# Splitting the fp16 parts of the expert weights into halves in a decoder layer

## The chip, the cores and the metric

The kernel runs on one core of a Trainium2 chip. Its time is the device time of one execution in microseconds (us); a lower one is better. The core has five engines that run side by side and wait for each other through semaphores: PE (matmul), ACT (activations), DVE (vector work), POOL and SP (which issues DMAs).

## The reference

One decoder layer over 8 sequences of 512 tokens, 256 wide: windowed self-attention, cross attention over a context, and a mixture of 8 experts of which each token uses 2. The change touches the work that lies in the second of them, cut here to its core with the experts behind it:

```python
scores = jnp.einsum('bqd,bkd->bqk', query, key)
scores = scores - tri[None, :, :]
probs = jax.nn.softmax(scores / SCALE, axis=-1)
return jnp.einsum('bqk,bkd->bqd', probs, value)
...
x = _layernorm(x + _L0_xattn_ref(x, ctx_1024, ctx_1024), axis=-1)
...
for e in range(NUM_EXPERTS):
    w_e = jnp.sum(jnp.where(top_i == e, routing_w, 0.0), axis=-1)
    h = jax.nn.gelu(xf @ expert_w1[e].T, approximate=False)
    out = out + h @ expert_w2[e].T * w_e[:, None]
```

## The kernel before

**Stages.** Window attention fills the first 525 us or so. Then comes the cross attention, one sequence b = 0 to 7 after another, some 18 us each (about 527 to 671 us of the profiled span). Behind it stand the routing (to about 715 us) and the experts, whose matmuls fill the rest.

**Expert weights.** The experts multiply in fp16 with each weight split in two: a high part, which is the scaled weight rounded to fp16, and a low part, which is what the rounding lost. There are 8 experts with two matrices each (k = 0 and 1), 2048 values to a partition in each. While the cross attention runs, SP loads them, ACT makes the high parts (`high_part`, L993, its instruction L999) and DVE the low parts (`low_part`, L1515, its instruction L1518). High and low of (e, k) lie in the memory of the loaded weights: the high part of (e, k) is written over the second half of the loaded (e, k-1), or of (e-1, 1). So `high_part(e, k)` waits on `w_low_made` until the low parts of all matrices before it are done (L998), and `low_part(e, k)` waits on `w_high_made` for its own high part.

**Order in a sequence.** No scheduler sets it: each engine runs its instructions in the order in which they are written. Sequences 2 to 5 run in a loop whose addresses are worked out in registers on the engine; 0, 1, 6 and 7 are written out.

- PE (`attend`, L639): scores of the four row blocks t = 0 to 3 (L646), with the transposes of the previous sequence's result (L686) ahead of t = 3; the router's product (L695); then for each t the transposes of the probabilities (L661) and, one block behind, the product with the context (L672). The product q = 2 uses the PSUM bank of q = 0 again, so it waits until the first residual sum has read it (L668).
- ACT (`attend`, L953): the high part of (b-2, 1), two copies (L1004, L1008), the exponentials of t = 0 and 1 (L963), the high part of (b-1, 0), the copy of the transposed probabilities of t = 0 (`copy`, L975), then exp(2), copy(1), exp(3), copy(2), copy(3), and two copies for the next sequence (L951).
- DVE (`attend`, L1472): masks (L1476), row peaks (L1480) and their scaling (`scale_peaks`, L1485), with the low part of (b-2, 1) between `scale_peaks(0)` and `mask(3)`; the choice of experts for sequence b-1 (`choose`, L1530 to L1539); the low part of (b-1, 0); the four residual sums, each a reciprocal (L1507), the sum (L1508) and the statistics (L1511); then eight tiny instructions, POOL's root (L1168) and the norm (L1524).

The four residual sums close a sequence: the norm follows the fourth, and PE, ACT and DVE all need the norm's result in the next sequence.

Of the kernel before, what the change touches and what calls it, by code (L numbers as in the profile page):

```python
# [16 lines left out]
ALU = mybir.AluOpType  # L17
# [30 lines left out]
N_EXP, TOP, F = 8, 2, 1024  # L48
FB = F // P
EW = C * F  # L50
PIECES = CHUNK
PIECE = N_EXP * EW // PIECES
F32_BIAS, F32_MANT = 127, 23
# [59 lines left out]
def past(t, k):  # L113

    return not isinstance(t, int) or t >= k
# [12 lines left out]
def decoder_layer(nc, x, x_steps, ctx, ctx_t, Wq, Wkv, q_g, q_b, k_g, k_b, Wwin, bwin, Wout,  # L128
                  router_t, w1_t, w2_t, shape_consts, out):
    stack = ExitStack()  # L130
    with stack:
# [3 lines left out]
        def sem(name):  # L135
            return stack.enter_context(nc.semaphore(name))
# [24 lines left out]
        def next_low(phase, *shape):  # L161
            start = low_used.get(phase, 0)
            n = 1
            for m in shape:
                n *= m
            low_used[phase] = start + n
            assert start + n <= LOW, (phase, start + n)
            return carve(low, start, *shape)
# [29 lines left out]
        where8 = next_low("cross", 2, QT, 8)  # L198
        assert low_used["cross"] <= LOW - EW // 2

# [36 lines left out]

        w_f32 = carve(big, 0, N_EXP, 2, EW)
        arena16 = arena[:, :].bitcast(F16)
        w_low = arena16[:, 2 * LOW:2 * LOW + 4 * N_EXP * EW].rearrange("p (e k x) -> p e k x", k=2, x=2 * EW)  # L240
        w_high = arena16[:, 2 * LOW - EW:2 * LOW - EW + 4 * N_EXP * EW].rearrange("p (e k x) -> p e k x", k=2, x=2 * EW)
# [5 lines left out]
        w_scale = carve(mid, scale_at, 8)  # L247
# [53 lines left out]
        w_piece = next_low("window", 2, PIECE)  # L301
        w_squares = next_low("window", 2, PIECES)
        w_sum = next_low("window", 2)
# [124 lines left out]
        w_high_made = sem("w_high_made")  # L428
        w_low_made = sem("w_low_made")
# [153 lines left out]
        def _(pe):  # L583
# [140 lines left out]
            nc.tensor.transpose(psum[0:TOP * TILES, 3, 0:P], top_v.rearrange("p k t -> p (k t)"), ident).then_inc(gates_turned, 1)  # L724

            pe.wait_ge(routed, 1)
            pe.wait_ge(w_low_made, 2 * N_EXP)

            def block_of(w, e, k, at, n):

# [69 lines left out]
        def _(act):  # L800
# [151 lines left out]

            def attend(b, u, i, more=True):  # L953
                if past(b, 2):
                    high_part(b - 2, 1)

                def exp(t):
                    act.wait_ge(peak_ready, 2 * b + t // (QT // 2) + 1)
                    if t >= 2:
                        act.wait_ge(pt_done, QT * b + t - 1)  # L960
                    elif past(b, 1):
                        act.wait_ge(pt_done, QT * b + t - 1)
                    nc.scalar.activation(probs[:, t % 2, 0:(t + 1) * P], psum[:, t, 0:(t + 1) * P], ACT.Exp,  # L963
                                         bias=bias2[:, u, t:t + 1], scale=1.0 / E ** 0.5,
                                         accum_out=row_sum[:, u, t:t + 1]).then_inc(exp2_done, 1)

                def copy(t):
                    act.wait_ge(pt_done, QT * b + t + 1)
                    if t < 2 and past(b, 1):
                        act.wait_ge(router_done, b)  # L970
                    if t >= 2:
                        act.wait_ge(av_done, QT * b + t - 1)
                    elif past(b, 1):
                        act.wait_ge(av_done, QT * b + t - 1)
                    nc.scalar.activation(probs_t[:, t % 2, 0:t + 1, :], psum[:, 4 + t % 2, 0:(t + 1) * P].rearrange(  # L975
                        "p (k n) -> p k n", n=P), ACT.Copy).then_inc(pt_copied, 1)
                if past(b, 1):
                    keep_x2(b - 1, 1 - u)
                    x2_transposed(b - 1)
                exp(0)  # L980
                exp(1)
                if past(b, 1):
                    high_part(b - 1, 0)
                copy(0)
                exp(2)
                copy(1)
                exp(3)
                copy(2)
                copy(3)
                if more:  # L990
                    copy_x1t(b + 1)

            def high_part(e, k):  # L993

                act.wait_ge(w_scaled, 1)
                act.wait_ge(w_loaded, 32 * e + 32)
                if k or past(e, 1):
                    act.wait_ge(w_low_made, 2 * e + k)  # L998
                nc.scalar.activation(w_high[:, bass.ds(e, 1), k, 0:EW], w_f32[:, bass.ds(e, 1), k, :],  # L999
                                     ACT.Copy, scale=w_scale[:, k:k + 1]).then_inc(w_high_made, 1)  # L1000

            def keep_x2(b, u):
                act.wait_ge(normed2, QT * (b + 1))
# [7 lines left out]
            steps(act, B - 2, attend)  # L1011
            attend(B - 2, 0, B // 2 - 1)
            attend(B - 1, 1, B // 2 - 1, more=False)
            high_part(N_EXP - 2, 1)
            keep_x2(B - 1, 1)
            x2_transposed(B - 1)
            high_part(N_EXP - 1, 0)
            high_part(N_EXP - 1, 1)


            nc.scalar.activation(count_psum, consts[:, AT_COUNT:AT_COUNT + P], ACT.Copy).then_inc(count_beside, 1)
# [213 lines left out]
        def _(dve):  # L1235
# [236 lines left out]
            def attend(b, u, i, more=True):  # L1472
                def mask(t):
                    dve.wait_ge(s_done, QT * b + t + 1)
                    diag = psum[:, t, t * P:(t + 1) * P]
                    nc.vector.tensor_tensor(diag, diag, consts[:, AT_MASK:AT_MASK + P], ALU.add).then_inc(masked, 1)  # L1476

                def find_peak(t):
                    dve.wait_ge(masked, QT * b + t + 1)
                    nc.vector.tensor_reduce(top_peak[:, u, t:t + 1], psum[:, t, 0:(t + 1) * P], op=ALU.max,  # L1480
                                            axis=AX.X).then_inc(peak_found2, 1)
                def scale_peaks(half):
                    part = slice(half * QT // 2, (half + 1) * QT // 2)
                    dve.wait_ge(peak_found2, QT * b + part.stop)
                    nc.vector.tensor_scalar(bias2[:, u, part], top_peak[:, u, part], -1.0 / E ** 0.5, None,  # L1485
                                            ALU.mult).then_inc(peak_ready, 1)
                mask(0)
                mask(1)
                if past(b, 1):
                    norm2(b - 1, 1 - u)  # L1490
                find_peak(0)
                find_peak(1)
                mask(2)
                scale_peaks(0)
                if past(b, 2):
                    low_part(b - 2, 1)
                mask(3)
                find_peak(2)
                find_peak(3)
                scale_peaks(1)  # L1500
                if past(b, 1):
                    choose(b - 1, 1 - u)
                    low_part(b - 1, 0)
                for t in range(QT):

                    dve.wait_ge(av_done, QT * b + t + 1)
                    done(nc.vector.reciprocal(inv_row[:, u, t:t + 1], row_sum[:, u, t:t + 1]), inv2_made, QT * b + t + 1)  # L1507
                    nc.vector.scalar_tensor_tensor(x1_n[:, u, t, :], psum[:, 6 + t % 2, 0:E], inv_row[:, u, t:t + 1],  # L1508
                                                   x1_n[:, u, t, :], ALU.mult, ALU.add).then_inc(sum2_done, 1)
                    dve.wait_ge(sum2_done, QT * b + t + 1)  # L1510
                    nc.vector.bn_stats(stats2[:, u, t, :], x1_n[:, u, t, :]).then_inc(stats2_done, 1)  # L1511
                dve.wait_ge(stats2_done, QT * (b + 1))
                moments(stats2[:, u], mean2[:, u, :], rstd2[:, u, :], b)

            def low_part(e, k):  # L1515

                dve.wait_ge(w_high_made, 2 * e + k + 1)
                nc.vector.scalar_tensor_tensor(w_low[:, bass.ds(e, 1), k, 0:EW], w_f32[:, bass.ds(e, 1), k, :], w_scale[:, k:k + 1],  # L1518
                                               w_high[:, bass.ds(e, 1), k, 0:EW], ALU.mult, ALU.subtract).then_inc(w_low_made, 1)

            def norm2(b, u):
                dve.wait_ge(rstd_ready, b + 1)
# [19 lines left out]
            attend(B - 2, 0, B // 2 - 1)  # L1542
            attend(B - 1, 1, B // 2 - 1, more=False)
            norm2(B - 1, 1)
            low_part(N_EXP - 2, 1)
            choose(B - 1, 1)


# [5 lines left out]
                                         count[:, 0:N_EXP].unsqueeze(1).unsqueeze(1).to_broadcast([P, TOP, TILES, N_EXP]),  # L1554
                                         ALU.is_equal), spot_step, 1)
            nc.vector.tensor_tensor(picked, chosen[:, 0], chosen[:, 1], ALU.add).then_inc(picked_made, 1)
            low_part(N_EXP - 1, 0)
            dve.wait_ge(counted, 1)
            tile_count = psum[:, 1, 0:TILES * N_EXP].rearrange("p (t n) -> p t n", n=N_EXP)

# [61 lines left out]
            half = SLOTS // 2  # L1622
# [50 lines left out]
            def result_out(s, v, i):  # L1673
                dve.wait_ge(down_done, s + 1)
                if past(s, 4):
# [2 lines left out]
                dve.wait_ge(y_beside, s + 1)  # L1678
                nc.vector.scalar_tensor_tensor(y_rows[:, v, :], psum[:, 6 + v % 2, 0:E], gate_col[:, v, :], y_side[:, v % 2, :],  # L1679
                                               ALU.mult, ALU.add).then_inc(y_copied, 1)  # L1680
            low_part(N_EXP - 1, 1)
            dve.wait_ge(routed, 1)
            quads(dve, SLOTS, lot, 8)
            result_out(SLOTS - 3, 1, SLOTS // 4 - 1)
# [54 lines left out]
```

## Time and profile before

| | us |
|---|---|
| three runs | 1202.16, 1204.65, 1205.75 |
| median | 1204.65 |
| the profiled execution | 1203.33 |
| its span | 1201.5 |
| PE / DVE / ACT / POOL busy in the span | 942.3 / 827.6 / 460.0 / 736.1 |
| 16 instructions of `high_part` | 2.00 each |
| 16 instructions of `low_part` | 2.35 each |

Times of rows are counted from the start of the span. The profiled execution took 1.8 us more than its span. The mean granted clock of TensorE over it was 0.92; two levels occur, 1.0 (2.4 GHz) and 0.5 (1.2 GHz).

How to read it: the busy times say little here, because no engine is busy throughout. What counts in each sequence is the chain of waits through PE, ACT and DVE.

### The profile page before, as it was taken

The page shows a single profiled execution, that of the slowest core. Times are in us where ns is not written, and L with a number is a line of the kernel's source. Part 1 is how long each engine was busy: PE and PEld are TensorE (multiplying, and loading weights), DVE is VectorE, ACT ScalarE, POOL GpSimd, SP SyncE. Part 2 cuts the span into 40 slices and gives each one's busy share as a digit, 9 for nine tenths or more (in the row PEclk, how much of TensorE's full clock was granted, in tenths as well). Part 3 has the DMA queues.
Part 4 walks back from the last instruction along what each step waited for, and adds up shares of the span by engine and source line. Part 5 has one row for each costly group of instructions (what it writes and reads, how often), then busy time and mean ns, then how long its engine had stood idle before and what let it go on. Part 6 is the DMA issues. An engine that isn't in the chain of part 4 may idle for free.

```text
span 1201.5 us, 24876 instructions
## 1 busy us (share of the span) xinstructions
PE 942.3 (78%) x8007; PEld 756.7 (63%) x8008; DVE 827.6 (69%) x1264; ACT 460.0 (38%) x1055; POOL 736.1 (61%) x496
## 2 busy tenths in 40 slices
PE   7984098888887887857878429999999999999940
PEld 4542087787787787835656317777777777777730
DVE  4899999999998998327888783444444444444435
ACT  3675223433444443435566312222333233223215
POOL 3575699999999999600000045666666666666522
PEclk9997599999998998979999669999999999999985
DMA  3362102121121221476775402222222222222236
GB/s 100 73 118 52 34 28 67 45 65 57 53 65 48 62 65 44 149 266 195 244 235 202 157 15 45 46 44 44 44 44 44 44 44 44 44 44 44 31 71 231
DMA packets 70136, 100.46 MB, mean 84 GB/s; under 512 B 9312, under 2 KB 51872, under 8 KB 69152
## 3 DMA queue, kind: packets, MB, share of 16 engines
q1 hardware_dynamic: 52816, 76.86, 20.6%
q0 software_dynamic: 16128, 18.93, 10.0%
q10 hardware_dynamic: 1152, 4.19, 0.9%
q8 instruction: 19, 0.31, 0.1%
q14 instruction: 21, 0.17, 0.0%
HBM read 73.96 MB, written 26.38 MB: 84 GB/s over the span
## 4 chain that ended last, share of the span: by engine, by line
PE 44%; POOL 23%; issue 14%; DVE 11%; DMA 4%; ACT 3%; POOLq 0%; SPq 0%; DVEq 0%; ACTq 0%
PE psum L744 17%; POOL mid L1142 13%; PE psum L752 11%; PE psum L754 5%; PE psum L672 3%; PE psum L595 2%; POOL arena L1147 2%; POOL arena L1155 2%; POOL arena L1133 1%; PE psum L736 1%; DMA sum_dram<-arena,mid 1%; PE psum L615 1%; DVE arena L1518 1%; PE psum L646 1%; POOL arena L1149 1%
## 5 line engine op out<-in xcount | busy, mean ns | idle before, releaser
L615 PE MATMUL psum<-consts,mid 128*128 128x128 f32 x2176 | 265.6, 286 | 87.6 <-POOL mid L1142 87.4
L615 PEld LDWEIGHTS psum<-consts,mid 128*128 128x128 f32 x2176 | 260.4, 201 | 99.0 <-issue 52.9
L744 PE MATMUL psum<-arena 128*128 128x128 f16 x3456 | 291.2, 220 | 5.1 <-issue 3.5
L744 PEld LDWEIGHTS psum<-arena 128*128 x3456 | 243.2, 98 | 76.9 <-issue 9.9
L1142 POOL TENSOR_TENSOR mid<-arena 128x2304 f32<-128x2304 f32 (+1 forms) x62 | 250.8, 4067 | 9.8 <-POOL arena L1133 7.6
L752 PE MATMUL psum<-arena 128*128 x576 | 218.1, 380 | 5.1 <-DVE arena L1670 1.2
L1222 POOL DMA_INDIRECT sum_dram<-arena,mid x72 | 142.5, 1980 | 46.1 <-issue 24.7
L1679 DVE SCALAR_TENSOR_TENSOR arena<-psum,arena 128x256 f32<-128x256 f32 x72 | 34.8, 484 | 190.1 <-ACT arena L1041 116.1
L754 PE MATMUL psum<-arena 128*128 x576 | 157.0, 273 | 0.0
L1381 DVE TENSOR_TENSOR mid<-psum,arena 128x4352 f32<-128x4352 f32 x32 | 149.8, 4683 | 0.6 <-issue 0.4
L1388 DVE TENSOR_REDUCE psum<-mid 128x272 f32<-128x4352 f32 x32 | 149.9, 4684 | 0.0
L1041 ACT ACTIVATE arena<-psum,arena 128x256 f32<-128x256 f32 x72 | 34.1, 473 | 301.8 <-PE psum L754 301.8
L1206 POOL DMA_INDIRECT arena<-x_dram,mid x72 | 75.3, 1045 | 102.0 <-PE psum L736 76.1
L1168 POOL TENSOR_TENSOR arena<-arena,minus_half 128x4 f32<-128x4 f32 x16 | 16.1, 1009 | 168.6 <-DVE arena L1249 168.6
L1670 DVE SCALAR_TENSOR_TENSOR arena<-arena,mid 128x1024 f16<-128x1024 f32 x72 | 92.5, 1285 | 2.6
L1214 POOL DMA_INDIRECT arena<-gate_dram,mid x72 | 72.0, 1001 | 21.9 <-issue 21.9
L1048 ACT ACTIVATE arena<-psum,mid 128x1024 f32<-128x1024 f32 x72 | 79.7, 1107 | 7.2 <-remote 4.8
L1669 DVE TENSOR_SCALAR arena<-arena,mid 128x1024 f16<-128x1024 f32 x72 | 54.3, 755 | 38.5 <-ACT arena L1048 37.2
L887 ACT ACTIVATE arena<-arena 128x512 f32<-128x512 f32 x64 | 39.8, 622 | 106.2 <-DMA arena<-w_t 106.2
L595 PE MATMUL psum<-arena,mid 128*128 128x512 f32 x128 | 64.0, 623 | 12.4 <-DMA arena<-Wwin 6.7
L1094 POOL TENSOR_TENSOR arena<-mid,arena 128x512 f32<-128x512 f32 x32 | 40.7, 1271 | 45.0 <-DVE mid L1262 44.9
L752 PEld LDWEIGHTS psum<-arena 128*128 128x128 f16 x576 | 56.0, 97 | 12.9 <-issue 10.3
(191 smaller groups left out, 1400.2 us busy)
## 6 DMA issues: line engine op xcount, KB each, us to landing
arena<-w_t SPq DMA_DIRECT2D x64, 256.0 KB, 2.8
arena<-w_t SPq DMA_DIRECT2D x16, 1024.0 KB, 10.4
arena<-x SPq DMA_DIRECT2D x32, 128.0 KB, 2.1
arena<-x_dram SPq DMA_DIRECT2D x8, 512.0 KB, 5.5
arena<-ctx_t SPq DMA_DIRECT2D x8, 512.0 KB, 6.3
arena<-ctx SPq DMA_DIRECT2D x8, 512.0 KB, 7.1
x_dram<-mid SPq DMA_DIRECT2D x8, 512.0 KB, 3.3
arena<-sum_dram SPq DMA_DIRECT2D x8, 512.0 KB, 4.9
```

Of the source, the lines that this page charges most:

```text
L595: nc.tensor.matmul(psum[:, u, :], x_step[:, quad % 2, at, c, :], w_in[:, c, 0:512], start=(c == 0), stop=(c == C - 1))
L615: last = nc.tensor.matmul(psum[:, u, c * P:(c + 1) * P], products[half][:, w, c * P:(c + 1) * P], ident, start=(a + w == 0 and c == 0), st ...
L744: last = nc.tensor.matmul(dst, block_of(w, e, 0, c * F + j * P, P), x[:, u, c * P:(c + 1) * P], start=(k == 0 and c == 0), stop=(k == 2 an ...
L752: nc.tensor.matmul(psum[:, 6 + u, :], hid_hi[:, u, j * P:(j + 1) * P], both, start=(j == 0), stop=False, skip_group_check=True)
L754: return nc.tensor.matmul(psum[:, 6 + u, E:2 * E], hid_lo[:, u, j * P:(j + 1) * P], high, start=False, stop=(j == FB - 1), skip_group_chec ...
L1048: nc.scalar.activation(hid[:, u, :].rearrange("p (h f) -> p h f", h=2), psum[:, 2 + 2 * u:4 + 2 * u, :], ACT.Gelu, scale=up_scale).then_in ...
L1142: nc.gpsimd.tensor_tensor(av_prod[half][:, :, :].rearrange("p w (h d) -> p w h d", d=D), values, weights, ALU.mult).then_inc(av_ready, 1)
L1206: nc.gpsimd.indirect_dma_start(rows[:, v, :], None, x2_dram, bass.IndirectOffsetOnAxis(slot_src[:, s:s + 1], 0)).then_inc(rows_loaded[v], 16)
L1222: nc.gpsimd.indirect_dma_start(sum_dram, bass.IndirectOffsetOnAxis(slot_dst[:, s:s + 1], 0), y_rows[:, v, :], None, compute_op=ALU.add).th ...
L1381: nc.vector.tensor_tensor(qk_prod[:, :].rearrange("p (w c) -> p w c", c=E), queries, k_all[:, bass.ds(t, K), :], ALU.mult).then_inc(qk_mul ...
L1388: nc.vector.tensor_reduce(raw.rearrange("p (h w) -> p w h", w=K), qk_prod[:, :].rearrange("p (w h d) -> p w h d", h=H, d=D), op=ALU.add, a ...
L1670: nc.vector.scalar_tensor_tensor(hid_lo[:, u, :], hid[:, u, :], hid_scale, hid_hi[:, u, :], ALU.mult, ALU.subtract).then_inc(hid_low, 1)
```

## The change

Each high and each low part is made by two instructions over 1024 values instead of one over 2048. `w_low_made` and `w_high_made` count halves. A half of a low part waits for its own half of the high part. The halves of a high part keep the wait for *all* low halves of the matrices before (L998, now with twice the number).

Their places change as well. On ACT the second half of the high part of (b-1, 0) stands between copy(1) and exp(3). On DVE the second half of the low part of (b-2, 1) stands behind `scale_peaks(1)`, and the halves of the low part of (b-1, 0) stand behind the first and the second residual sum, where the whole part stood ahead of the first. The other parts are made by two halves in a row.

```diff
+HALF = EW // 2
...
-            pe.wait_ge(w_low_made, 2 * N_EXP)
+            pe.wait_ge(w_low_made, 4 * N_EXP)
...
                 if past(b, 2):
-                    high_part(b - 2, 1)
+                    high_parts(b - 2, 1)
...
                 exp(0)
                 exp(1)
                 if past(b, 1):
-                    high_part(b - 1, 0)
+                    high_part(b - 1, 0, 0)
                 copy(0)
                 exp(2)
                 copy(1)
+                if past(b, 1):
+                    high_part(b - 1, 0, 1)
                 exp(3)
...
-            def high_part(e, k):
+            def high_part(e, k, half):
...
                 if k or past(e, 1):
-                    act.wait_ge(w_low_made, 2 * e + k)
...
+                    act.wait_ge(w_low_made, 2 * (2 * e + k))
+                part = slice(half * HALF, (half + 1) * HALF)
...
                 scale_peaks(0)
                 if past(b, 2):
-                    low_part(b - 2, 1)
+                    low_part(b - 2, 1, 0)
                 mask(3)
                 find_peak(2)
                 find_peak(3)
                 scale_peaks(1)
+                if past(b, 2):
+                    low_part(b - 2, 1, 1)
                 if past(b, 1):
                     choose(b - 1, 1 - u)
-                    low_part(b - 1, 0)
                 for t in range(QT):
...
+                    if t < 2 and past(b, 1):
+                        low_part(b - 1, 0, t)
...
-            low_part(N_EXP - 1, 1)
+            low_parts(N_EXP - 1, 1)
```

ACT in sequence 7, before: L963 is an exponential, L975 a copy, L999 the high part.

```order
L963 ACTIVATE arena<-psum,arena 128x256 [waits pt_done,peak_ready]
L999 ACTIVATE arena<-arena,mid 128x2048 [waits w_low_made,w_loaded,w_scaled]
L975 ACTIVATE arena<-psum 128x128 [waits av_done,router_done,pt_done]
L963 ACTIVATE arena<-psum,arena 128x384 [waits pt_done,peak_ready]
L975 ACTIVATE arena<-psum 128x256 [waits av_done,router_done,pt_done]
L963 ACTIVATE arena<-psum,arena 128x512 [waits pt_done,peak_ready]
```

The same place after the change, where the high part is L1003, the exponential L964 and the copy L976.

```order
L964 ACTIVATE arena<-psum,arena 128x256 [waits pt_done,peak_ready]
L1003 ACTIVATE arena<-arena,mid 128x1024 [waits w_low_made,w_loaded,w_scaled]
L976 ACTIVATE arena<-psum 128x128 [waits av_done,router_done,pt_done]
L964 ACTIVATE arena<-psum,arena 128x384 [waits pt_done,peak_ready]
L976 ACTIVATE arena<-psum 128x256 [waits av_done,router_done,pt_done]
L1003 ACTIVATE arena<-arena,mid 128x1024 [waits w_low_made,w_loaded,w_scaled]
L964 ACTIVATE arena<-psum,arena 128x512 [waits pt_done,peak_ready]
```

The second half has moved behind the second copy and ahead of the last exponential; both halves carry the wait on `w_low_made`.

DVE in sequence 7, before: scaling of the peaks (L1485), low part of (5, 1) (L1518), mask(3) and peaks, the choice of experts (L1530 to L1539), low part of (6, 0), first sum.

```order
L1485 TENSOR_SCALAR arena<-arena 128x2 [waits peak_found2]
L1518 SCALAR_TENSOR_TENSOR arena<-arena,mid 128x2048 [waits w_high_made]
L1476 TENSOR_TENSOR psum<-psum,consts 128x128 [waits s_done]
L1480 TENSOR_REDUCE arena<-psum 128x1 [waits masked] x2
L1485 TENSOR_SCALAR arena<-arena 128x2 [waits peak_found2]
L1530 COPY arena<-psum 128x32 [waits router_done]
...
L1539 CAST mid<-arena 128x2x4
L1518 SCALAR_TENSOR_TENSOR arena<-arena,mid 128x2048 [waits w_high_made]
L1507 RECIPROCAL arena<-arena 128x1 [waits av_done]
```

After the change, with the low halves as L1532, the peaks' scaling L1493, the choice from L1548 to L1557, and the reciprocal of a sum L1516.

```order
L1532 SCALAR_TENSOR_TENSOR arena<-arena,mid 128x1024 [waits w_high_made]
L1484 TENSOR_TENSOR psum<-psum,consts 128x128 [waits s_done]
L1488 TENSOR_REDUCE arena<-psum 128x1 [waits masked] x2
L1493 TENSOR_SCALAR arena<-arena 128x2 [waits peak_found2]
L1532 SCALAR_TENSOR_TENSOR arena<-arena,mid 128x1024 [waits w_low_made,w_high_made]
L1548 COPY arena<-psum 128x32 [waits router_done]
...
L1557 CAST mid<-arena 128x2x4
L1516 RECIPROCAL arena<-arena 128x1 [waits av_done]
L1517 SCALAR_TENSOR_TENSOR arena<-psum,arena 128x256 [waits inv2_made]
L1520 BN_STATS arena<-arena 128x6 [waits sum2_done]
L1532 SCALAR_TENSOR_TENSOR arena<-arena,mid 128x1024 [waits w_high_made]
L1516 RECIPROCAL arena<-arena 128x1 [waits av_done]
```

The low part of (5, 1) now ends behind the second scaling of the peaks, and nothing stands between the choice of experts and the first sum; the first half of (6, 0) follows that sum.

## Rows read from the trace of the kernel before

**Rows 1.** Page: chain that ended last, share of the span by engine.
```profile
PE 44%; POOL 23%; issue 14%; DVE 11%; DMA 4%; ACT 3%; POOLq 0%; SPq 0%; DVEq 0%; ACTq 0%
```

**Rows 2.** That chain in order of time: start us, us, what.
```profile
537.73 0.44 PE psum L661 x4
...
608.24 2.35 DVE arena L1518
...
611.33 1.53 PE psum L672 x6
...
683.55 2.26 DVE arena L1518
```

**Rows 3.** Instructions of lines 999 and 1518: ns min/median/max, first and last start.
```profile
L999 ACT ACTIVATE arena<-arena,mid x16: 1992/2002/2007, 549.4 to 685.9; 128x2048 f16<-128x2048 f32 x8, - x8
...
L1518 DVE SCALAR_TENSOR_TENSOR arena<-arena,mid x16: 2343/2348/2353, 552.8 to 714.3; 128x2048 f16<-128x2048 f32 x8, - x8
```

**Rows 4.** Page, costliest groups: the same DVE operation over 1024 values.
```profile
L1670 DVE SCALAR_TENSOR_TENSOR arena<-arena,mid 128x1024 f16<-128x1024 f32 x72 | 92.5, 1285 | 2.6
```

**Rows 5.** Timeline of sequence 4: start, us, engine, line, operation [idle before <-releaser].
```profile
601.50 1.06 ACT L1004 ACTIVATE mid<-arena 128x1024 f32 x1 [1.72 <-DVE arena L1524]
...
602.32 2.35 DVE L1518 SCALAR_TENSOR_TENSOR arena<-arena,mid  x1 [0.16 <-issue]
602.34 1.88 PE L646 MATMUL psum<-arena 128*128 128x512 f32 x4
...
604.59 0.29 DVE L1476 TENSOR_TENSOR psum<-psum,consts 128x128 f32<-128x128 f32 x1
...
604.90 2.00 ACT L999 ACTIVATE arena<-arena,mid  x1 [0.53 <-DVE arena L1518]
...
605.97 0.17 DVE L1485 TENSOR_SCALAR arena<-arena 128x2 f32<-128x2 f32 x1
...
606.80 0.26 ACT L975 ACTIVATE arena<-psum 128x128 f32<-128x128 f32 x1
...
607.11 0.70 PE L672 MATMUL psum<-arena 128*128 128x256 f32 x2 [0.83 <-ACT arena L975]
...
607.78 0.70 ACT L963 ACTIVATE arena<-psum,arena 128x512 f32<-128x512 f32 x1
...
608.24 2.35 DVE L1518 SCALAR_TENSOR_TENSOR arena<-arena,mid  x1 [0.22 <-issue]
...
610.51 0.16 DVE L1507 RECIPROCAL arena<-arena 128x1 f32<-128x1 f32 x1
...
611.33 1.53 PE L672 MATMUL psum<-arena 128*128 128x256 f32 x6 [1.81 <-DVE arena L1508]
...
611.57 0.15 DVE L1507 RECIPROCAL arena<-arena 128x1 f32<-128x1 f32 x1
...
615.07 0.16 DVE L1507 RECIPROCAL arena<-arena 128x1 f32<-128x1 f32 x1 [1.02 <-PE psum L672]
```

**Rows 6.** Timeline of sequence 1, which is written out: same columns.
```profile
551.25 0.28 ACT L975 ACTIVATE arena<-psum 128x128 f32<-128x128 f32 x1
...
552.76 2.34 DVE L1518 SCALAR_TENSOR_TENSOR arena<-arena,mid 128x2048 f16<-128x2048 f32 x1
...
559.58 0.16 DVE L1507 RECIPROCAL arena<-arena 128x1 f32<-128x1 f32 x1 [1.02 <-PE psum L672]
```

**Rows 7.** Windows in sequences 3 and 6: last PEclk, DMA share, GB/s.
```profile
590.00:592.00 2.00, 2.00 (x7) 1.53 (x7) 2.00 (x1) 0.63 (x3) 0.00 (x0) 0.50 1.05 387
...
644.00:646.00 2.00, 2.00 (x7) 1.50 (x7) 1.97 (x8) 1.63 (x6) 0.00 (x0) 0.50 0.98 354
```

**Rows 8.** Timeline of sequence 7, written out: columns as in Rows 5.
```profile
661.29 0.26 ACT L975 ACTIVATE arena<-psum 128x128 f32<-128x128 f32 x1
...
668.87 0.16 DVE L1507 RECIPROCAL arena<-arena 128x1 f32<-128x1 f32 x1 [0.58 <-PE psum L672]
```

**Rows 9.** Timeline where the experts begin.
```profile
719.60 0.69 PE L736 MATMUL psum<-consts,arena 128*128 128x128 f32 x2 [6.40 <-DMA arena<-x_dram,mid]
```

More of the change, by code:

```diff
@@ L997, in high_part, with high_parts @@
                 if k or past(e, 1):
-                    act.wait_ge(w_low_made, 2 * e + k)
-                nc.scalar.activation(w_high[:, bass.ds(e, 1), k, 0:EW], w_f32[:, bass.ds(e, 1), k, :],
+                    act.wait_ge(w_low_made, 2 * (2 * e + k))
+                part = slice(half * HALF, (half + 1) * HALF)
+                nc.scalar.activation(w_high[:, bass.ds(e, 1), k, part], w_f32[:, bass.ds(e, 1), k, part],
                                      ACT.Copy, scale=w_scale[:, k:k + 1]).then_inc(w_high_made, 1)
+            def high_parts(e, k):
+                high_part(e, k, 0)
+                high_part(e, k, 1)
             def keep_x2(b, u):
@@ L1013, in _ @@
             attend(B - 1, 1, B // 2 - 1, more=False)
-            high_part(N_EXP - 2, 1)
+            high_parts(N_EXP - 2, 1)
             keep_x2(B - 1, 1)
             x2_transposed(B - 1)
-            high_part(N_EXP - 1, 0)
-            high_part(N_EXP - 1, 1)
+            high_parts(N_EXP - 1, 0)
+            high_parts(N_EXP - 1, 1)
             nc.scalar.activation(count_psum, consts[:, AT_COUNT:AT_COUNT + P], ACT.Copy).then_inc(count_beside, 1)
@@ L1511, in attend, with low_part, low_parts @@
                     nc.vector.bn_stats(stats2[:, u, t, :], x1_n[:, u, t, :]).then_inc(stats2_done, 1)
+                    if t < 2 and past(b, 1):
+                        low_part(b - 1, 0, t)
                 dve.wait_ge(stats2_done, QT * (b + 1))
                 moments(stats2[:, u], mean2[:, u, :], rstd2[:, u, :], b)
[L1515 to L1519, printed above, removed]
+            def low_part(e, k, half):
+                dve.wait_ge(w_high_made, 2 * (2 * e + k) + half + 1)
+                if half:
+                    dve.wait_ge(w_low_made, 2 * (2 * e + k) + 1)
+                part = slice(half * HALF, (half + 1) * HALF)
+                nc.vector.scalar_tensor_tensor(w_low[:, bass.ds(e, 1), k, part], w_f32[:, bass.ds(e, 1), k, part], w_scale[:, k:k + 1],
+                                               w_high[:, bass.ds(e, 1), k, part], ALU.mult, ALU.subtract).then_inc(w_low_made, 1)
+            def low_parts(e, k):
+                low_part(e, k, 0)
+                low_part(e, k, 1)
             def norm2(b, u):
@@ L1544, in _ @@
             norm2(B - 1, 1)
-            low_part(N_EXP - 2, 1)
+            low_parts(N_EXP - 2, 1)
             choose(B - 1, 1)
@@ L1556, in _ @@
             nc.vector.tensor_tensor(picked, chosen[:, 0], chosen[:, 1], ALU.add).then_inc(picked_made, 1)
-            low_part(N_EXP - 1, 0)
+            low_parts(N_EXP - 1, 0)
             dve.wait_ge(counted, 1)
```

## The prediction

> **What bounds the kernel now.** I read the chain that ended last first. By engine, PE has 44% of it and DVE 11% [rows 1], so DVE is not the bound of the kernel, but its pieces count where they stand on that chain. The second view is the chain in order of time, inside the cross attention. In sequence 4 it runs from the low part on DVE (608.24 us, 2.35 us) to the product q = 2 on PE (611.33 us) [rows 2]. The third is the timeline of that sequence. PE had waited 1.81 us for the first residual sum before that product [rows 5]: the sum stood behind the low part. That is the wait which the change attacks. What the reader should look at beside it is the ACT row at 604.90 us: the high part had waited 0.53 us for a low part on DVE, and copy(0), exp(2), copy(1) and exp(3) are queued behind it, on which PE waits. So a second chain runs close to the first, and it starts at the low part that is now moved later.
>
> **The prices.** A whole high part takes 2.00 us and a whole low part 2.35 us [rows 3]. For the low half the nearest row is the same DVE operation over 1024 values, 1.28 us [rows 4]; the lower bound is half of 2.35, 1.17 us. I take 1.28, since that row has the same operands. For the high half, an ACT copy over 1024 values took 1.06 us [rows 5]; the lower bound is 1.00. I take 1.06. An instruction starts about 0.08 to 0.10 us before the one ahead of it ends (mask(3) at 604.59 against 604.67; copy(0) at 606.80 against 606.90), so a high half between two others costs 0.96. In the loop a low part has an issue pause of 0.16 to 0.22 us ahead of it [rows 5]; each half gets one there, and none in the sequences that are written out.
>
> The Trainium skill ("VectorE: DVE Perf Modes", section "The TRN2 errata — SBUF-src ops pay a fixed extra latency per instruction") speaks against such a split: a large tile pays the latency once, small tiles pay it each time, and the measured fixed term there is about 150 cycles. That would be an estimated 0.16 us for each added low instruction, where the two rows give 2 x 1.28 - 2.35 = 0.22; with it a sequence with two halves between the sums would come out 0.1 to 0.2 us shorter.
>
> **Sequences 2 to 5, worked on sequence 4** [rows 5]. (1) DVE: the first half of the low part of (2, 1) starts at 602.32 and ends at 603.60. mask(3) then waits for the scores only, which end at 602.34 + 1.88 = 604.22; it starts near 604.30, 0.3 us earlier than before. The second scaling follows 1.38 later, at 605.68 (604.59 to 605.97 before). Then the second half: 605.68 + 0.17 + 0.16 = 606.01, to 607.29. (2) ACT: the first high half of (3, 0) has to wait until all low halves before it are made, so until 607.29. The hand-over took 0.23 before (604.67 to 604.90): it starts at 607.52, and copy(0) at 607.52 + 0.96 = 608.48, against 606.80. That is 1.68 later, although only half of the work stands ahead of it. (3) exp(3) started 0.98 behind copy(0); now the second high half lies between, so 608.48 + 0.98 + 0.96 = 610.42, and ends at 611.12. With a hand-over of about 0.1 and the 0.44 that the transposes held PE before the next product in sequence 0 [rows 2], q = 2 starts at 611.66, against 611.33: 0.33 later, and the fourth sum would be 0.33 later too. (4) DVE again: the choice of experts takes 606.14 to 608.02, 1.88 us; it now ends at 609.17. The first product of the probabilities moves with copy(0): 607.11 + 1.68 = 608.79, ends 609.49, and the first sum starts at 609.5, against 610.51. A sum lasts 1.06 (610.51 to 611.57). With a low half behind it, 1.06 + 0.08 + 0.22 + 1.28 - 0.08 = 2.56. So the fourth starts at 609.5 + 2 x 2.56 + 1.06 = 615.68, against 615.07: **0.61 later**. This is the later of the two chains and sets the norm and the next sequence. The gain at the first sum (1.0 us) is spent twice, by the late start of copy(0) and by the halves which now lie between sums that had none.
>
> Sequences 2, 4 and 5 get 0.61 each, 1.8 together. In sequence 3 the granted clock was 0.50 around 591 us [rows 7]; the first product is then up to 0.35 longer than its 0.70. That gives 0.6 to 1.0; I take 0.8.
>
> **Sequences 6 and 7**, written out, without issue pauses. The same steps (1) and (2) give copy(0) about 1.67 later [rows 8]: the scores end close to the low part there, so no 0.3 us are won, but the 0.16 pause and half of the 0.23 hand-over are missing. First sum: 661.29 + 1.67 + 0.31 + 0.70 = 663.97. A sum with its half lasts 2.26; the fourth starts at 663.97 + 4.52 + 1.06 = 669.55, against 668.87: 0.68 later. For both, 1.4.
>
> **Sequence 1** has no low part of (b-2, 1), and its first high half waits for nothing. There the change does what it is written for: the first sum starts where the low part started, 552.76, and the fourth at 552.76 + 4.52 + 1.06 = 558.34, against 559.58 [rows 6]: 1.24 earlier. PE is ready by then: copy(0) stays at 551.25, exp(3) ends at 553.9 and q = 2 can start at 554.5.
>
> **The rest.** The low part of (7, 0) stands on the chain at 683.55 [rows 2], and there are two instructions for one: 0.2. The low part of (7, 1) ends just before the experts; PE waited 6.40 us for the first rows until 719.60 [rows 9], which hides its 0.2. Without that cover it would cost these 0.2. The halves of (b-2, 1) on ACT at a sequence's start lie in ACT's wait for the norm (1.72 us ahead of L1004 [rows 5]) and cost nothing. DMAs are issued in the same order and behind the same sums.
>
> Sum: -1.24 + 1.8 + 0.8 + 1.4 + 0.2 = **+3.0 us**. On the profiled execution, 1203.33, that is 1206.3. That execution lies 1.3 below the median of the three runs, 1204.65. I forecast against the median: **1207.6**. About 0.3% (3.6 us) is what a measurement can tell from no change, so this forecast stands just inside it.
>
> **The rivals.**
> (A) *The slow clock comes out of its cover.* Before, the stretches at 0.50 in sequences 3 and 6 [rows 7] lay where PE had time: up to 1.81 us of waiting ahead of q = 2. By the sum above PE reaches the fourth product only 0.35 us ahead of DVE, so a longer PE phase shows at once. PE also waits 1.7 us longer for copy(0), and if the clock falls in four more sequences, each with about 1.0 us of its products uncovered, the time is 3.0 + 4 = 7.0 us above, 1211.6. It decides from 0.6 us of uncovered PE time on. Against it: the same PE work stays inside the same period. The Trainium skill ("TensorE: Matmul & The Clock Gate", section "What's actually happening") says the throttled state is the default and activity releases it, which speaks for this one. Chance 0.21.
> (B) *The late low half does not hold ACT.* If the high half of (b-1, 0) could start as early as before, all seven sequences would gain what sequence 1 gains: 7 x -1.24 + 0.2 = -8.5, 1196.2. For it: sequence 1. Against it: the wait counts every half before, and the half of (b-2, 1) stands behind `scale_peaks(1)`. Chance 0.07.
> (C) *Cheap halves.* With 1.17 per half and no pauses in the loop, a sum with its half lasts 2.15; the fourth sum is then bound by ACT and PE, about 0.2 late in the loop and 0.4 in the other two, and sequence 1 gains 1.46: 0.8 + 0.8 - 1.46 + 0.1 = 0.2, 1204.9. Chance 0.17.
>
> **How the numbers follow.** The forecast has 0.55; its own range, 1206 to 1209.5, lies on both sides of the bound of 3.6 us, and I give 0.33 of it to "same" and 0.22 to slower. With (C) "same" has 0.50; with (A) slower has 0.43; faster is (B), 0.07. The range goes from (C), rounded down, to (A): 1204.0 to 1211.6, which leaves out (B) and the far side of (A).
>
> **What the profile of the changed kernel would show.** In sequence 4, counted from the product of the scores of t = 3: a low half behind the second scaling; the first high half waiting for it, with over 2 us idle on ACT; copy(0) about 1.7 later; the first sum about 1 us earlier; PE's wait ahead of q = 2 now for ACT's copy or exponential and not for L1508's successor; and the fourth sum released by DVE's own halves with no wait for PE. Sequence 1 shorter by 1.2 us, sequences 2 to 7 longer by 0.6 to 0.8. I am wrong if ACT's first high half does not wait for the low half, if the half on DVE takes far from 1.28, or if the granted clock in 545 to 671 differs from before.

## The result and the profile after

The changed kernel takes **1215.16 us** (median of 4 runs, 1213.65 to 1216.31), against 1205.2 for the kernel before (median of 4, 1202.16 to 1206.12). The ratio is 1.0086 with a 95% interval of 1.0064 to 1.0109: it is 10 us slower. The prediction was 1207.6 with a range of 1204.0 to 1211.6, so the time lies outside it.

The chain that ended last, share of the span by engine, answers to [rows 1]. PE has 45%, which says as little as before.

```profile
PE 45%; POOL 22%; issue 14%; DVE 10%; DMA 4%; ACT 3%; POOLq 0%; SPq 0%; ACTq 0%; DVEq 0%
```

The same chain in order of time, of the changed kernel in sequence 4, answers to [rows 2]. L1532 is a low half, L673 a product of the probabilities, L662 their transposes.

```profile
607.70 1.30 DVE arena L1532
610.57 1.22 PE psum L673 x2
611.79 0.64 PE psum L662 x3
612.43 1.71 PE psum L673 x4
614.14 0.85 PE psum L662 x4
614.99 1.52 PE psum L673 x6
```

Before, the chain went from the low part of (3, 0) to the first residual sum and to q = 2. Now it goes from the second half of the low part of (2, 1), through ACT's first high half and copy(0), to PE, and stays on PE from q = 0 to q = 3.

Where the time went is seen by stage. The windows of both kernels begin and end at different work, so I use POOL's root of each sequence (L1168 before, L1176 after) as the mark. Its start in sequence 0 and in sequence 7 is at 544.03 and 671.23 us before, at 542.74 and 681.79 after. The cross attention between these marks takes 127.20 and 139.05 us: **+11.85**. Outside of it the two executions differ by 1.4 us the other way, nearly all of it ahead of sequence 0, where nothing is changed.

| root to root, us | 1 | 2 | 3 | 4 | 5 | 6 | 7 | sum |
|---|---|---|---|---|---|---|---|---|
| before | 17.91 | 18.55 | 18.44 | 18.50 | 18.45 | 17.90 | 17.45 | 127.20 |
| after | 16.60 | 20.66 | 20.56 | 20.52 | 20.50 | 20.27 | 19.94 | 139.05 |

Sequence 1 is 1.31 us shorter, as forecast (1.24). The other six are 2.0 to 2.5 us longer each, where 0.6 to 0.8 was forecast.

The instructions of the high half (L1003) and the low half (L1532) of the changed kernel answer to [rows 3] and [rows 4]: ns min/median/max, first and last start, and below each what its engine sat idle for (us, times).

```profile
L1003 ACT ACTIVATE arena<-arena,mid x32: 1132/1147/1156, 548.1 to 697.9; 128x1024 f16<-128x1024 f32 x16, - x16
...
  DVE arena L1532: 26.7, 8
```
```profile
L1532 DVE SCALAR_TENSOR_TENSOR arena<-arena,mid x32: 1268/1284/1286, 552.5 to 726.6; 128x1024 f16<-128x1024 f32 x16, - x16
```

A low half takes the 1.28 us taken for it, so halving a low part costs 2 x 1.284 - 2.348 = 0.22 us. A high half takes 1.15, not 1.06. ACT waits 26.7 us for low halves in 8 waits; that was 10.0 in 8 before.

The timeline of sequence 4 of the changed kernel answers to [rows 5].

```profile
605.89 0.30 DVE L1484 TENSOR_TENSOR psum<-psum,consts 128x128 f32<-128x128 f32 x1 [0.63 <-PE psum L647]
...
607.70 1.28 DVE L1532 SCALAR_TENSOR_TENSOR arena<-arena,mid  x1 [0.25 <-issue]
...
609.21 1.15 ACT L1003 ACTIVATE arena<-arena,mid  x1 [3.21 <-DVE arena L1532]
...
610.26 0.26 ACT L976 ACTIVATE arena<-psum 128x128 f32<-128x128 f32 x1
...
610.57 1.22 PE L673 MATMUL psum<-arena 128*128 128x256 f32 x2 [2.65 <-ACT arena L976]
...
611.83 0.16 DVE L1516 RECIPROCAL arena<-arena 128x1 f32<-128x1 f32 x1 [0.95 <-PE psum L673]
...
614.17 0.16 DVE L1516 RECIPROCAL arena<-arena 128x1 f32<-128x1 f32 x1
...
614.78 1.73 PE L673 MATMUL psum<-arena 128*128 128x256 f32 x6
...
618.72 0.16 DVE L1516 RECIPROCAL arena<-arena 128x1 f32<-128x1 f32 x1 [1.02 <-PE psum L673]
```

The first five of these rows are the chain that was forecast: the mask goes as soon as the scores are there, the second low half follows, ACT waits 3.21 us for it, copy(0) comes late and PE has waited 2.65 us, where it had waited 0.83. Counted from POOL's root (598.93 before, 600.56 after), copy(0) starts at 9.70 instead of 7.87. The fourth sum is released by PE, after a wait of 1.02 us as before, and not by DVE's halves. Before, PE itself had waited for DVE ahead of q = 2; now it does not, and its products are slow: the first takes 1.22 us instead of 0.70. The windows of the changed kernel around it say why; the third number from the right is the granted clock, as in [rows 7].

```profile
608.00:610.00 2.00, 0.00 (x0) 0.00 (x0) 1.71 (x10) 0.79 (x1) 0.00 (x0) 0.62 1.03 355
610.00:612.00 2.00, 1.43 (x4) 1.14 (x5) 0.86 (x8) 2.00 (x6) 0.00 (x0) 0.50 1.09 397
612.00:614.00 2.00, 2.00 (x8) 1.52 (x7) 1.94 (x3) 1.44 (x4) 0.00 (x0) 0.50 1.02 401
614.00:616.00 2.00, 2.00 (x10) 1.83 (x9) 1.93 (x5) 0.60 (x1) 0.00 (x0) 0.67 1.04 358
```

PE does nothing in the first window and the clock falls to 0.50 (1.2 GHz) in it, at 608.5 us, where PE's last work ended at 607.9; the products after it run at that level until about 615 us. The same happens in each of sequences 2 to 7. Before, the clock fell in sequences 3 and 6 alone, and in sequence 3 not in a wait: it fell at about 589.4 us, with PE at work again since 588.69 behind a wait of 0.84 us. Its row and the window around it, of the kernel before:

```profile
588.69 0.70 PE L672 MATMUL psum<-arena 128*128 128x256 f32 x2 [0.84 <-ACT arena L975]
```
```profile
588.00:590.00 2.00, 1.31 (x6) 1.05 (x7) 1.46 (x15) 2.00 (x7) 0.00 (x0) 0.83 1.01 207
```

Over 545 to 671 us the mean granted clock of the changed kernel is 0.86, against 0.97 before; the prediction had named a difference there as a sign that it is wrong.

### The profile page after: what moved, and what is told of

Its sections match the earlier page's. It is cut to its first block, busy times and chain, and to the rows that moved or that the text cites. A ratio compares the mean times of both kernels' runs of the same rounds, so it can differ in the third digit from the quotient of the medians.

```text
span 1211.9 us, 24972 instructions
## 1 busy us (share of the span) xinstructions
PE 952.7 (79%) x8007; PEld 765.7 (63%) x8008; DVE 831.4 (69%) x1280; ACT 462.8 (38%) x1071; POOL 735.2 (61%) x496
## 4 chain that ended last, share of the span: by engine, by line
PE 45%; POOL 22%; issue 14%; DVE 10%; DMA 4%; ACT 3%; POOLq 0%; SPq 0%; ACTq 0%; DVEq 0%
PE psum L745 17%; POOL mid L1150 13%; PE psum L753 11%; PE psum L755 5%; PE psum L673 3%; PE psum L596 2%; POOL arena L1155 2%; PE psum L737 2%; POOL arena L1163 2%; PE psum L647 2%; POOL arena L1141 1%; PE psum L616 1%; DVE arena L1532 1%; POOL arena L1157 1%; ACT arena L1077 1%
## 5 line engine op out<-in xcount | busy, mean ns | idle before, releaser
L1176 POOL TENSOR_TENSOR arena<-arena,minus_half 128x4 f32<-128x4 f32 x16 | 16.1, 1009 | 180.9 <-DVE arena L1257 180.9
```

## The experiments

Four theories were set against each other; the numbers are those of the expectations: (1) the late second low half holds ACT, PE idles, and its clock falls; (2) halves between the residual sums cost the time; (3) the halves' order on ACT costs it; and, without a number, that the clock costs nothing beyond the wait. All edits below are to the changed kernel where nothing else is said.

| kernel | us | ratio to before, 95% interval | sequences 1 to 7, us |
|---|---|---|---|
| changed | 1215.16 | 1.0086 (1.0064 to 1.0109) | 139.05 |
| pair of halves early | 1196.89 | 0.9939 (0.992 to 0.9957) | 120.86 |
| 8 added matmuls | 1209.09 | 1.0037 (1.0025 to 1.0049) | 133.10 |
| 5 added matmuls | 1204.91 | 1.0007 (0.9996 to 1.0018) | 129.68 |
| 2 added matmuls | 1204.27 | 1.0021 (1.0005 to 1.0038) | 132.35 |
| before, whole low part late | 1226.72 | 1.018 (1.0162 to 1.0197) | 150.82 |
| before, halves only | 1212.66 | 1.006 (1.004 to 1.0079) | 136.73 |
| halves only, 3 matmuls ahead of q = 0 | 1211.26 | 1.0073 (1.005 to 1.0096) | 136.66 |
| halves only, 3 matmuls ahead of q = 2 | 1210.41 | 1.0064 (1.0044 to 1.0084) | 137.38 |
| before, 2 added matmuls | 1202.31 | 0.9983 (0.9971 to 0.9996) | 127.16 |
| whole low part early | 1194.74 | 0.9921 (0.9907 to 0.9935) | 119.02 |
| only the low halves behind the sums | 1196.07 | 0.9925 (0.9911 to 0.9939) | 120.11 |

The last column is one profiled execution each. The added matmuls do not touch sequence 1, and yet it takes 16.60 us in the changed kernel with none and with 5, but 17.46 with 8 and with 2: in these two traces the clock is at 0.50 in it for about 3 us, between 554 and 559 us. So 0.86 us of their sums is a slow stretch that the edit did not make.

### The second low half put back ahead of mask(3)

```diff
                 if past(b, 2):
-                    low_part(b - 2, 1, 0)
+                    low_parts(b - 2, 1)
                 mask(3)
...
-                if past(b, 2):
-                    low_part(b - 2, 1, 1)
```

> The changed kernel with one edit: both halves of the low part of (b-2, 1) stand ahead of mask(3), where the whole part stood before. Theory 1 (the late second low half holds ACT's high half, PE then idles 2.65 us, its clock falls to 0.50 in sequences 2 to 7): ACT's wait of 3.21 us falls under 1 us, the slow stretch in sequences 2 to 7 is gone or as rare as before (2 of 7), and each of these sequences is about 1.0 us shorter than before, as sequence 1 is; in all about 7 us under the kernel before, 1197 to 1199 us. Theory 2 (halves between the residual sums cost the time themselves, on DVE): the time stays at 1213 to 1216 us. Theory 3 (the order of high halves on ACT costs it): between, about 1206 us.

1196.89 us, just under the range: 18 us under the changed kernel by one moved half, and 8 us under the kernel before. Its timeline in sequence 4:

```profile
604.34 1.15 ACT L1003 ACTIVATE arena<-arena,mid  x1 [1.12 <-DVE arena L1530]
...
605.83 0.67 PE L673 MATMUL psum<-arena 128*128 128x256 f32 x2 [0.68 <-DVE arena L1546]
...
607.38 0.15 DVE L1514 RECIPROCAL arena<-arena 128x1 f32<-128x1 f32 x1
...
613.08 0.14 DVE L1514 RECIPROCAL arena<-arena 128x1 f32<-128x1 f32 x1
```

ACT's wait is 1.12 us instead of 3.21 (under 1 was expected), PE's 0.68 instead of 2.65; the product takes 0.67 again. The row of the product names DVE's L1546, the copy of the router's result, which PE also needs: it ended at 605.68, just behind copy(0) at 605.66. A slow stretch is left in one sequence, the second. The mean granted clock of this kernel between 545 and 666 us is 0.99. Theories (2) and (3) fall: the halves between the sums and the halves on ACT are all still there. The fourth sum starts 5.70 us behind the first, where it was 4.56 before (610.51 to 615.07 in [rows 5]), and yet the sequence is shorter, since the first sum comes that much earlier.

### The whole low part moved late, with nothing halved

An edit to the kernel before:

```diff
                 scale_peaks(0)
-                if past(b, 2):
-                    low_part(b - 2, 1)
                 mask(3)
                 find_peak(2)
                 find_peak(3)
                 scale_peaks(1)
+                if past(b, 2):
+                    low_part(b - 2, 1)
```

> The kernel before with one edit: the whole low part of (b-2, 1) stands behind the second scaling of the peaks, no part is halved. Theory 1: ACT's high part of (b-1, 0) waits over 3 us, PE idles over 3.5 us, the clock falls in all of sequences 2 to 7, and since a whole low part (2.35) and a whole high part (2.00) now stand in a row ahead of copy(0), the time is 18 to 24 us over the kernel before, 1223 to 1229 us. Theory 2 (the halves cost it): within 3 us of the kernel before.

1226.72 us. The order alone, without a single half, does more harm than the change. The waits of 545 to 700 us in this kernel: us in total, times, longest.

```profile
PE psum L672 <- ACT arena L975: 26.7, 7, 4.6
ACT arena L999 <- DVE arena L1518: 24.7, 6, 4.3
```

PE waits up to 4.6 us at a time for copy(0). Sequences 2 to 7 take 21.1 to 23.0 us, and all have a slow stretch.

### Matmuls that fill PE's wait

They separate the wait from the clock: all waits of the changed kernel stay, PE is only kept busy through its own. The added matmuls write half a PSUM bank that nothing reads.

```diff
+                    if t == 1 and past(b, 2):
+                        for _ in range(8):
+                            nc.tensor.matmul(psum[:, 6, E:2 * E], ident, ctx_sb[:, u, 0, :], start=True, stop=True,
+                                             skip_group_check=True)
                     if t:
                         q = t - 1
                         pe.wait_ge(pt_copied, QT * b + q + 1)
```

> The changed kernel, all its waits kept, with 8 added matmuls of 128x256 in sequences 2 to 7 on PE ahead of the product q = 0, where PE now idles; they write an unused half bank and nothing reads them. Theory 1 with the clock as the larger part: the granted clock stays at 1.0 in these sequences, each is 1.3 to 1.5 us shorter than in the changed kernel, and the time is 1205 to 1208 us, where the sum of the prediction put it (+3). If the clock costs nothing beyond the wait (a rival), it stays at 1213 to 1216 us.

1209.09 us, just above the range named. The 8 matmuls, 16 passes in the record, run too long:

```profile
610.20 3.62 PE L667 MATMUL psum<-arena,consts 128*128 128x256 f32 x16
...
612.70 0.26 ACT L980 ACTIVATE arena<-psum 128x128 f32<-128x128 f32 x1
...
613.65 0.59 PE L677 MATMUL psum<-arena 128*128 128x256 f32 x2
```

copy(0) is done at 612.96, and the product starts 0.7 later behind the added work. Of the 3.42 us by which its seven sequences exceed those with 5 matmuls (below), 0.86 are the slow stretch in sequence 1. So the count was cut to 5.

> The changed kernel with 5 added matmuls on PE in sequences 2 to 7 in place of 8, which nothing reads. The 8 ran for 3.62 us and ended 0.65 us after copy(0) was made, so they held up the product they stood ahead of; 5 take 2.3 us and end before it. If the clock is the whole difference between the wait's own price (the prediction's +3) and the measured +10, the granted clock is near 1.0 in sequences 2 to 7 and the time is 1205 to 1208 us, 1 to 4 us below the kernel with 8. If the wait's own price is larger than reckoned, it stays at 1208 to 1210 us.

**1204.91 us.** Five matmuls that compute nothing bring the changed kernel back to the time of the kernel before (1204.35 on the same chip). Its timeline in sequence 4:

```profile
604.61 2.32 PE L667 MATMUL psum<-arena,consts 128*128 128x256 f32 x10
...
606.06 1.15 ACT L1007 ACTIVATE arena<-arena,mid  x1 [3.20 <-DVE arena L1536]
...
607.42 0.70 PE L677 MATMUL psum<-arena 128*128 128x256 f32 x2 [0.49 <-ACT arena L980]
...
608.16 0.16 DVE L1520 RECIPROCAL arena<-arena 128x1 f32<-128x1 f32 x1 [0.44 <-PE psum L677]
...
610.45 1.46 PE L677 MATMUL psum<-arena 128*128 128x256 f32 x6
...
614.12 0.16 DVE L1520 RECIPROCAL arena<-arena 128x1 f32<-128x1 f32 x1 [0.17 <-PE psum L677]
```

ACT's wait is the same, 3.20 us. The product takes 0.70 us. The mean granted clock over 545 to 671 us is 1.00:

```profile
545.00:671.00 126.00, 109.08 (x586) 82.76 (x586) 104.25 (x350) 75.55 (x138) 6.04 (x6) 1.00 0.60 205
```

against this row of the changed kernel:

```profile
545.00:671.00 126.00, 100.86 (x499) 77.51 (x499) 98.13 (x331) 69.83 (x127) 6.04 (x6) 0.86 0.60 204
```

Its sequences take 16.60, 19.07, 19.06, 19.06, 19.06, 18.63 and 18.20 us. So the clock costs 139.05 - 129.68 = **9.4 us** in the changed kernel, 1.4 to 1.7 a sequence, and the late wait with the halves costs what is left against before, 129.68 - 127.20 = **2.5 us**: 3.8 more in sequences 2 to 7, less the 1.3 that sequence 1 gains.

With 2 matmuls instead of 5:

> The changed kernel with 2 added matmuls (0.9 us) instead of 5 in PE's wait of 2.65 us, which nothing reads. It asks how much of the wait must be filled. If any work in the wait keeps the clock, 1203 to 1207 us as with 5; if the clock still falls, 1212 to 1216 us as without; if it falls in some sequences, between, with loop sequences of either 19.1 or 20.5 us in the trace.

1204.27 us (the kernel before 1203.32 there), in two groups: six executions of 1202.89 to 1204.48 and four of 1207.54 to 1208.76. The profiled one, 1207.81, is of the second group and showed the third case: sequences 2 and 4 with a slow stretch (20.19 and 19.73 us), the others in the loop 19.07, the last two 18.63 and 18.20 as with 5. Sequence 1, which has no added matmuls, had one too. That the first group has fewer stretches is likely and not shown, since none of it was traced.

The control, 2 matmuls (`range(2)`) in the kernel before:

> The kernel before with 2 added matmuls (0.9 us) at the same place in sequences 2 to 7, which nothing reads: the control for the added matmuls. Its slow stretches in sequences 3 and 6 lay where PE had time, so keeping them away gains nothing: within 2 us of the kernel before. If slow stretches cost time there too, 1 to 4 us less than before.

1202.31 us, ratio 0.9983 (0.9971 to 0.9996). In its trace the slow stretches of sequences 3 and 6 are gone and the seven sequences take 127.16 us, against 127.20: a slow stretch that lies where PE waits anyway costs nothing. Sequence 1 of this trace has one (553 to 556 us) and takes 17.92 us, against 17.91 without; in the changed order, where that wait is gone, a stretch as long cost 0.86. The 2 us between the medians do not come from there, and are about as small as can be told.

### Halves only, in the old order

Every part of the kernel before is made by two halves in a row, nothing is moved.

```diff
                     choose(b - 1, 1 - u)
+                    low_parts(b - 1, 0)
                 for t in range(QT):
...
-                    if t < 2 and past(b, 1):
-                        low_part(b - 1, 0, t)
```

(and `high_parts(b - 1, 0)` ahead of copy(0), `low_parts(b - 2, 1)` ahead of mask(3)).

> The kernel before with each high and low part made by two halves in a row at its old place; no order is changed. From the measured halves (1.147 us on ACT, 1.284 us on DVE; 2 x 1.147 - 2.00 = 0.29 and 2 x 1.284 - 2.35 = 0.22) two low halves and two high halves stand in the chain of a sequence: 0.4 to 0.5 us each for sequences 2 to 7 and 0.2 for the end, 2 to 3 us over the kernel before, 1207 to 1208 us. If the split was the cause of the loss (Theory 2), 8 us or more.

1212.66 us, 7.9 over before: far more than the 2 to 3 that I expected. The timeline shows one cause:

```profile
608.38 1.28 DVE L1527 SCALAR_TENSOR_TENSOR arena<-arena,mid  x1 [0.19 <-issue]
...
610.02 1.28 DVE L1527 SCALAR_TENSOR_TENSOR arena<-arena,mid  x1 [0.35 <-DVE arena L1527]
...
611.52 2.19 ACT L1001 ACTIVATE arena<-arena,mid  x2 [1.12 <-DVE arena L1527]
...
618.54 2.69 PE L673 MATMUL psum<-arena 128*128 128x256 f32 x6 [2.21 <-DVE arena L1514]
```

The second half waits for the first one's semaphore, and in the loop the pair starts 1.64 us apart: it takes 2.92 us where one instruction takes 2.35, 0.57 more and not 0.22. Two such pairs lie in the chain of a sequence: +1.15, which gives the 19.6 to 19.7 us of loop sequences 3 and 5. But sequences 2 and 4 took 21.4. There the product q = 2, behind PE's wait of 2.21 us, ran at 0.50 (2.69 us instead of 1.53). Sequences 3 and 5 have a slow stretch as well, which the next expectation passes over: it lies earlier, on the transposes and the product q = 1 (595 to 598 us in sequence 3), and PE's wait ahead of q = 2 shrinks to 0.80 and 0.55 us and pays for it.

> The kernel with halves only (old order, each part two halves in a row) plus 3 added matmuls (1.4 us) on PE in sequences 2 to 7, which nothing reads. Its trace showed loop sequences of 21.4 us with a slow stretch and 19.6 to 19.7 without, and pairs of low halves that take 2.92 us in the loop. If the clock is one part and the dependent pair the other, all loop sequences take 19.6 to 19.7 us, so 1.1 to 1.2 us over the kernel before each, and the time is 1208 to 1210 us, 3 to 4 under the kernel with halves only. If the pair explains all, it stays at 1212 us.

1211.26 us: the expectation failed. The loop sequences took 21.39, 19.72, 21.37 and 19.58 us as before. The matmuls stood ahead of q = 0. They did take the stretches out of sequences 3 and 5, which had cost nothing; those of sequences 2 and 4 began in the wait ahead of q = 2 and stayed. So the matmuls were put there, into bank 4 behind the wait on the third copy:

> The kernel with halves only, with 3 added matmuls (1.4 us, read by nothing) ahead of the product q = 2 in sequences 2 to 7, where PE waits 2.2 us for the first sum, and none ahead of q = 0. The kernel with 3 of them ahead of q = 0 did not get faster; its slow stretches began in this second wait and lay on the products q = 2 and q = 3, in every other loop sequence (21.4 against 19.6 us). If that reading is right, all four loop sequences take 19.5 to 19.8 us and the time is 1207 to 1210 us. If the 21.4 us have another cause, they stay and the time is 1210 to 1213 us.

1210.41 us, and that failed too, though sequences 2 and 4 did what was expected. The product after the filled wait kept its 1.56 us, and the loop sequences took 19.64, 21.18, 19.61 and 21.26: the slow stretches are gone from sequences 2 and 4 and costly in the other two (sequence 7, 19.13 us, has one too); in sequence 3 it begins at 589 to 590 us, in the wait ahead of q = 0. This kernel has two waits of PE in a sequence, of 1.6 and 2.2 us. Filling one leaves the other. That both together would remove it is argued and was not tried; why it begins in one wait in sequences 2 and 4 and around the other in 3 and 5 stays open.

### What is left of the change when its harm is taken out

Both kernels have the whole low part of (b-2, 1) ahead of mask(3), by one instruction; the second also has whole high parts in the sequences.

```diff
                 if past(b, 2):
-                    low_part(b - 2, 1, 0)
+                    whole_low(b - 2, 1)
...
-                    high_part(b - 1, 0, 0)
+                    whole_high(b - 1, 0)
...
-                if past(b, 1):
-                    high_part(b - 1, 0, 1)
```

> The kernel with the pair of low halves of (b-2, 1) ahead of mask(3), but made by one instruction of 2048 values. Two dependent halves in a row started 1.64 us apart in the loop, so the pair took 2.92 us and one takes 2.35: 0.57 us less ahead of ACT's high half and of the first sum, in 6 sequences. Theory 1 expects 3 us under the kernel with the pair, 1193 to 1195 us. If the residual sums are bound by something else, it stays at 1196 to 1198 us.

> As the kernel with the whole low part early, but the high parts inside the sequences are whole too and stand where they stood before (ahead of copy(0)); of the change only the two low halves behind the first and second sum are left. The first sum then waits for the choice of experts (its end at 608.0 in the row numbers of sequence 4 of the kernel before) and hardly for copy(0) (606.8): Theory 1 expects the same as with halved high parts, 1193 to 1196 us. If the halves on ACT carry the gain, 1200 us or more.

1194.74 and 1196.07 us, ratios of 0.9921 and 0.9925: the same within their intervals, and both 8 to 10 us under the kernel before (1196.07 is 0.07 over its range). The first is the fastest kernel of this study. Its loop sequences take 17.1 us (one of them 17.5), against 17.6 to 17.9 with the pair of halves; those of the second take 17.95, 17.34, 17.06 and 17.11, the first of them with a slow stretch. So the gain of the change is in the two low halves behind the first and second residual sum; the halves of the high part add nothing that can be told. Not tried was the whole low part of (b-1, 0) behind the first sum: how much of the gain is the later place and how much the halving stays open.

## Why the prediction was wrong

**The chain was right.** ACT's first high half waits for the second low half, copy(0) comes late, the first sum comes early, sequence 1 gains. The kernel with 5 added matmuls has all of this at full clock, and there the sum can be compared term by term: sequences 2 to 5 cost 0.52, 0.62, 0.56 and 0.61, where the sum had 0.61 each and 0.8 in sequence 3; sequences 6 and 7 cost 0.73 and 0.75, where it had 0.68; sequence 1 gains 1.31, where it had 1.24. Together +2.5 against +2.8 for these stages. That it comes so close is partly luck, as the next lines show.

**Some of its terms were off, and cancelled.** The high half was taken as 1.06 us from a copy of 1024 fp32 values; it takes 1.15. Two of them stand ahead of the product q = 2, which starts 0.63 later (13.03 us behind the root instead of 12.40), not 0.33: they explain somewhat over half of the 0.30, the hand-overs on ACT and PE the rest. The sum with its half was taken as 2.56 us, with an issue pause of 0.22; it took 2.32 (608.16 to 610.48), without a visible pause. So the fourth sum is released by PE, with 0.17 us of waiting, and not by DVE. The sum had DVE's chain 0.61 late and PE's 0.33; it was PE's that ended late and set the 0.6. (By that sum PE is 0.28 us ahead of DVE, not the 0.35 that rival (A) names.)

**The step that failed is the clock.** The sum carried the clock of the kernel before over into the changed one: two stretches at 0.50 in seven sequences. But one of its own terms was that PE waits 1.7 us longer for copy(0), and this wait is where the stretch now begins in each of sequences 2 to 7. Rival (A) named this mechanism and had 0.21; its argument against itself, that the same PE work stays inside the same period, did not hold: PE's work per period was kept and the clock fell all the same, in the empty part of the period. Its price was wrong too: 1.0 in four more sequences, where it is 1.4 to 1.6 us in each of the four in the loop and 1.6 and 1.7 in the last two, 9.4 in all. What decides in which period the clock falls is not shown: in the kernel before, with waits of 0.5 to 1.8 us, it fell in two of six sequences. A slow stretch had cost nothing before (127.16 against 127.20 with and without) because q = 2 waited for DVE anyway; the change removed that cover, as (A) said.

By the Trainium skill ("TensorE: Matmul & The Clock Gate", section "What's actually happening") the throttled state is the default and activity releases it; the trace agrees: PE is idle at 608 to 610 us with 0.62 in that window, and back at 1.0 from about 615 us, with PE at work since 610.57.

**Rival (B)** fell in the changed kernel, and its arithmetic held roughly where its condition was made true: with the pair early all seven sequences gain, 6.3 us in sum, and with the whole part early 8.2, where it had 8.7. **Rival (C)** fell with the measured half of 1.28, though its other parts came true: no pauses behind the sums, and a fourth sum bound by ACT and PE. The rest of the sum held: between the last root and the first gather of expert rows there are 43.8 us instead of 43.5 (forecast +0.2).

## What to carry to other kernels

When a moved step makes TensorE wait longer, look at the granted clock of the products behind that wait: here 1.8 us more of waiting in each of six sequences cost 3.8 us by itself and 9.4 us through the clock, and a handful of matmuls that compute nothing gave the 9.4 back. Before a step is moved later, look for who waits on its semaphore: half of a low part was moved off DVE's way to the last mask and into the wait of ACT, which feeds the sums, and putting it back turned a loss of 10 us into a gain of 8 to 10. Of a change in several parts, test each alone; here one part held the gain and another the loss.

## What was not expected of the hardware

Two dependent DVE halves in a row in a loop started 1.64 us apart, though each takes 1.28; where the instructions are written out they started 1.40 apart (2.68 us a pair), and the halves behind the sums, with other work between them, started without a visible gap. And by filling one of two waits of 1.6 and 2.2 us the costly slow stretches were moved, not removed, while in the changed kernel, which has one long wait, 5 matmuls (2.3 us) removed all of them and 2 matmuls all but two.
